# Value products in one piece behind an up group, both value copies ahead of the gelu

## The reference

```
h = layernorm(x) * (1 + ca) + sa
q = h @ w_dq.T @ w_uq.T;  k, v = split(h @ w_dkv.T @ w_ukv.T)      # 16 heads of 16
p = softmax(q @ k.T / 4 + causal mask)
x = x + ga * (p @ v) @ w_out.T
h = layernorm(x) * (1 + cb) + sb
expert 0: gelu(h @ W0a.T + b0a) @ W0b.T + b0b;  expert 1: relu(h @ W1a.T + b1a) @ W1b.T + b1b
x = x + gb * (the output of the expert with the larger gate score, token by token)
```

## Time and profile before

| | |
|---|---|
| three runs | 595.57, 596.92, 600.63 us; median 596.92 |
| profiled execution | 593.84 us, span of the trace 592.1 us |
| TensorE | 515.4 us busy (87%), 4912 matmuls |
| VectorE | 480.8 us (81%), 949 instructions |
| ScalarE | 366.5 us (62%), 521 |
| GpSimd | 311.9 us (53%), 300 |
| granted TensorE clock, mean | 0.951 |

### The profile page before, as it was taken

One profiled execution on the slowest core, in us unless ns is written; L12 is line 12 of the kernel. 1 busy time (PEld: TensorE's weight loads), 2 busy tenths in 40 slices (PEclk: granted clock), 3 DMA queues, 4 the chain that ended last, 5 costly groups with the idle time before them and its releaser, 6 DMA issues.

```text
span 592.1 us, 14257 instructions
## 1 busy us (share of the span) xinstructions
PE 515.4 (87%) x4912; PEld 446.2 (75%) x4912; DVE 480.8 (81%) x949; ACT 366.5 (62%) x521; POOL 311.9 (53%) x300
## 2 busy tenths in 40 slices
PE   4534685989999999999999999999999999999974
PEld 4424463788888988888888888788988898888874
DVE  3538163779999899989898989999899999887573
ACT  1524464858585866667676858585766667676320
POOL 6235232455656665755646565656665665552441
PEclk9856598899999999999999999999999999999998
DMA  8835453262707080716244351708080615210100
GB/s 246 206 46 76 50 74 75 52 95 37 128 18 145 2 161 3 121 42 90 71 68 93 50 111 31 130 7 154 0 152 13 108 39 91 55 39 2 37 19 18
DMA packets 43802, 43.74 MB, mean 74 GB/s; under 512 B 5344, under 2 KB 40800, under 8 KB 43760
## 3 DMA queue, kind: packets, MB, share of 16 engines
q1 hardware_dynamic: 43760, 43.19, 39.1%
HBM read 13.39 MB, written 4.23 MB: 30 GB/s over the span
## 4 chain that ended last, share of the span: by engine, by line
PE 49%; DVE 19%; DMA 10%; issue 9%; SPq 5%; POOL 3%; ACT 3%; DVEq 0%; POOLq 0%; ACTq 0%
DMA qs<-parts_q 8%; PE ps_s L382 6%; DVE mx L933 6%; PE ps_t L401 5%; PE ps_o L419 3%; PE ps_a L333 3%; PE ps_t L405 3%; SPq L282 3%; PE ps_a L334 3%; PE ps_a L335 3%; PE ps_c L333 3%; PE ps_c L335 2%; PE ps_c L334 2%; PE ps_o L333 2%; POOL xs L1186 2%
## 5 line engine op out<-in xcount | busy, mean ns | idle before, releaser
L794 ACT ACTIVATE score_rows<-ps_s 128x1024 f32<-128x1024 f32 x96 | 98.8, 1030 | 79.3 <-PE ps_s L382 66.2
L1246 POOL TENSOR_SCALAR_AFFINE_SELECT score_rows<-score_rows 128x512 f32<-128x512 f32 (+1 forms) x96 | 80.0, 834 | 110.4 <-ACT score_rows L794 109.8
L933 DVE TENSOR_REDUCE mx<-score_rows 128x4 f32<-128x1024 f32 (+1 forms) x96 | 114.6, 1210 | 5.7 <-POOL score_rows L1246 5.5
L806 ACT ACTIVATE p<-ps_t 128x1024 f32<-128x1024 f32 x96 | 98.5, 1026 | 17.9 <-PE ps_t L405 17.3
L382 PE MATMUL ps_s<-ks,qs 96*128 96x256 bf16 (+1 forms) x512 | 63.3, 260 | 33.2 <-DMA qs<-parts_q 29.7
L382 PEld LDWEIGHTS ps_s<-ks,qs 96*128 96x128 bf16 x512 | 37.0, 103 | 47.9 <-DMA qs<-parts_q 23.2
L1186 POOL TENSOR_TENSOR xs<-z,xs 128x512 f32<-128x512 f32 (+1 forms) x16 | 34.9, 2182 | 68.7 <-DVE z L1022 68.7
L401 PE MATMUL ps_t<-qs,ks 99*128 99x256 bf16 (+1 forms) x512 | 61.1, 254 | 11.0 <-DMA qs<-mx_rows 10.3
L401 PEld LDWEIGHTS ps_t<-qs,ks 99*128 99x128 bf16 x512 | 38.8, 101 | 17.5 <-DMA qs<-mx_rows 6.3
L405 PE MATMUL ps_t<-past_b,ident_b 128*128 128x256 bf16 (+1 forms) x192 | 46.0, 322 | 0.0
L1234 POOL TENSOR_TENSOR hid_lo<-hid,hid_hi 128x512 fp32r<-128x512 f32 x32 | 42.8, 1350 | 4.8 <-DVE hid_hi L1092 4.8
(11 more groups left out here) (166 smaller groups left out, 1631.4 us busy)
## 6 DMA issues: line engine op xcount, KB each, us to landing
qs<-parts_q SPq DMA_DIRECT2D x96, 128.0 KB, 4.0
ks<-parts_k SPq DMA_DIRECT2D x96, 128.0 KB, 4.7
xs<-x SPq DMA_DIRECT2D x16, 256.0 KB, 4.1
gates<-gates_scratch SPq DMA_DIRECT2D x16, 256.0 KB, 4.5
out<-xs SPq DMA_DIRECT2D x16, 256.0 KB, 2.9
p<-wmod SPq DMA_DIRECT2D x1, 1024.0 KB, 6.7
p<-waT SPq DMA_DIRECT2D x1, 1024.0 KB, 9.1
p<-wmod SPq DMA_DIRECT2D x1, 512.0 KB, 5.9
```

Of the source, the lines that this page charges most:

```text
L794: act.activation(score_rows[c % 2][:], ps_s[:], ACT.Copy).then_inc(scores_out, 1)
L806: act.activation((p0, p1)[tile][:, h0:h0 + n, :], ps_t[:].rearrange("p (h s) -> p h s", h=n), ACT.Exp, scale=SCALE).then_inc(exp_done, 1)
L933: dve.tensor_reduce(dst, score_rows[c % 2][:].rearrange("p (h k) -> p h k", h=n), AX_X, ALU.max).then_inc(max_done, 1)
L1246: pool.affine_select(out=diag, in_=diag, compare_op=ALU.is_ge, fill=NEG, base=0, pattern=[[0, n], [-1, P]], channel_multiplier=1).then_inc ...
```

## The change

- `values` becomes one stage of all 16 heads. It waits for v and for all six chunks of exponentials, and writes group g to columns g * 256 to g * 256 + 255 of the two banks of `ps_t`, instead of `ps_o`. `pv_done` counts 2 for a batch (after groups 1 and 3), before 4.
- On TensorE it stands behind `up(at(3), 0)`. Before, groups 0 and 1 stood on both sides of `s_chunk` 5 ahead of `expand_k`, and groups 2 and 3 behind up 0. `st_chunk` 0 of the next batch now also waits for both value copies (`o_ready`).
- On ScalarE `k_first` comes ahead of the copies, and both `values_copy` follow at the end of the step, so that the second one is ahead of the next step's `gelu` 0, which it followed before.
- The lists of users of `ps_o` are shortened, and its memset at the start goes away.

```diff
                 if c == 0:
                     pe.wait_ge(maxrows_in, 16 * (b.n + 1))
+                    wait(pe, o_ready, 2 * b.n)
...
-            def values(b, g, *users):
+            def values(b):
...
-                if g == 0:
-                    pe.wait_ge(v_ready, b.n + 1)
-                pe.wait_ge(exp_done, CH * b.n + ST_OF_GROUP[g])
-                bank_left(users)
-                for n in range(4):
-                    h = 4 * g + n
-                    dst = BANK["PVa"][32 * n:32 * n + HD + 1, (g % 2) * S:(g % 2 + 1) * S]
-                    pe.matmul(dst, v[b.parity][:, 0, h, :], p0[:, h, :], start=True, stop=False)
-                    mm = pe.matmul(dst[:, P:S], v[b.parity][:, 1, h, :], p1[:, h, :], start=False, stop=True)
-                mm.then_inc(pv_done, 1)
+                pe.wait_ge(v_ready, b.n + 1)
+                pe.wait_ge(exp_done, CH * (b.n + 1))
+                for g in range(4):
+                    for n in range(4):
+                        h = 4 * g + n
+                        dst = ps_t[32 * n:32 * n + HD + 1, g * S:(g + 1) * S]
+                        pe.matmul(dst, v[b.parity][:, 0, h, :], p0[:, h, :], start=True, stop=False)
+                        mm = pe.matmul(dst[:, P:S], v[b.parity][:, 1, h, :], p1[:, h, :], start=False, stop=True)
+                    if g % 2 == 1:
+                        mm.then_inc(pv_done, 1)
...
                 st_chunk(at(2), 5)
-                values(at(2), 0, ("DN0", at(4)), ("UP3", at(4)), ("V", at(1)))
                 s_chunk(at(1), 5)
-                values(at(2), 1)
                 expand_k(at(0), ("CKV", at(0)))
                 up(at(3), 0, ("Q", at(0)), ("T2", at(3)))
-                values(at(2), 2, ("PVa", at(2)))
-                values(at(2), 3)
+                values(at(2))
                 up(at(3), 1, ("DN1", at(4)), ("T1", at(0)))
...
             def step(at):
                 gelu(at(4), 0)
-                values_copy(at(3), 1)
                 maxima_rows(at(2))
...
                 scores_copy(at(1), 5)
+                k_first(at(0))
                 values_copy(at(2), 0)
-                k_first(at(0))
+                values_copy(at(2), 1)
                 rest_of_weights(at(0))
...
-            dve.memset(ps_o[:], 0.0).then_inc(blank, 1)
```

More of the change, by code:

```diff
@@ L210, in block_kernel @@
         BANK = dict(T1=ps_a, Q=ps_c, CKV=ps_b, K=ps_b, V=ps_o, MT=ps_c, OT0=ps_o, OT1=ps_b, AT=ps_b, OP=ps_c, T2=ps_c,
-                    GT=ps_a, GX=ps_b, UP0=ps_c, UP1=ps_a, UP2=ps_c, UP3=ps_o, DN0=ps_o, DN1=ps_a, PVa=ps_o, PVb=ps_o)
+                    GT=ps_a, GX=ps_b, UP0=ps_c, UP1=ps_a, UP2=ps_c, UP3=ps_o, DN0=ps_o, DN1=ps_a)
         LAGS = 4
@@ L340, in _ @@
                 "K": ((k1_ready, 1, 1), (kr_ready, 1, 1)), "V": ((v_ready, 1, 1),), "MT": ((mt_ready, 1, 1),),
-                "PVa": ((o_ready, 2, 1),), "PVb": ((o_ready, 2, 2),), "OT0": ((attn_ready, 2, 1),), "OT1": ((attn_ready, 2, 2),),
+                "OT0": ((attn_ready, 2, 1),), "OT1": ((attn_ready, 2, 2),),
                 "AT": ((a_hi_ready, 1, 1), (a_lo_ready, 1, 1)), "OP": ((gated_ready, 1, 1),), "T2": ((g32_ready, 1, 1),),
@@ L603, in _ @@
             pe.wait_ge(consts_ready, 6)
-            pe.wait_ge(blank, 4)
+            pe.wait_ge(blank, 3)
             pe.wait_ge(z1_ready, 1)
@@ L618, in step @@
                 turn_maxima(at(2), ("UP0", at(4)), ("Q", at(1)))
-                turn_values(at(3), 0, ("PVb", at(3)))
+                turn_values(at(3), 0, ("DN0", at(5)), ("UP3", at(5)), ("V", at(2)), ("OT0", at(4)))
                 turn_values(at(3), 1, ("K", at(1)), ("CKV", at(1)), ("GX", at(5)))
                 up(at(4), 2, ("MT", at(2)), ("UP0", at(4)))
-                expand_v(at(1), ("OT0", at(3)), ("PVb", at(3)), ("PVa", at(3)), ("DN0", at(5)), ("UP3", at(5)), ("V", at(2)))
+                expand_v(at(1), ("OT0", at(3)), ("DN0", at(5)), ("UP3", at(5)), ("V", at(2)))
                 gate(at(4), ("UP1", at(4)))
@@ L625, in step @@
                 st_chunk(at(2), 0)
-                up(at(4), 3, ("V", at(1)), ("OT0", at(3)), ("PVb", at(3)), ("PVa", at(3)), ("DN0", at(5)))
+                up(at(4), 3, ("V", at(1)), ("OT0", at(3)), ("DN0", at(5)))
                 project_out(at(3), ("UP2", at(4)), ("MT", at(2)))
@@ L685, in values_copy @@
                     return
-                act.wait_ge(pv_done, 4 * b.n + 2 * half + 2)
+                act.wait_ge(pv_done, 2 * b.n + half + 1)
                 wait(act, ot_done, 2 * b.n)
-                act.activation(oT[:, 2 * half:2 * half + 2, :], BANK["PVa"][:].rearrange("p (g s) -> p g s", g=2), ACT.Copy).then_inc(o_ready, 1)
+                act.activation(oT[:, 2 * half:2 * half + 2, :], ps_t[:, half * 512:(half + 1) * 512].rearrange("p (g s) -> p g s", g=2), ACT.Copy).then_inc(o_ready, 1)
             def second_expert(b, t):
@@ L763, in v_copy @@
                 act.wait_ge(v_done, b.n + 1)
-                wait(act, pv_done, 4 * (b.n - 1))
+                wait(act, pv_done, 2 * (b.n - 1))
                 act.activation(v[b.parity][:, :, :, 0:HD], BANK["V"][:].rearrange("p (t h e) -> p t h e", t=TT, h=NH), ACT.Copy).then_inc(v_ready, 1)
@@ L799, in exponentials @@
                 act.wait_ge(st_done, CH * b.n + c + 1)
-                wait(act, pv_done, 4 * (b.n - 1) + (2, 1, 2, 4, 3, 4)[c])
+                wait(act, pv_done, 2 * (b.n - 1) + (1, 1, 1, 2, 2, 2)[c])
                 if b.first and c == 0:
```

## The result

The changed kernel takes 622.2 us (median of 4 runs, 616.9 to 623.71) against 596.9: 1.040 times the kernel before, 95% interval 1.032 to 1.048, slower. The forecast was 612.9 and slower, with a range of 602 to 622: the direction is as forecast, and the time lies at the upper end of the range, 0.2 us beyond it. The profiled execution took 616.9 us, span 615.1, against 593.84: +23.1 us. The ten periods from the fourth start of mx_rows on are 33.58 us each on average, 31.87 before: +1.71 us.

The account below looks back on a forecast made before the run. VectorE's and TensorE's balanced loops were taken to bound the kernel, VectorE's stall deciding: 11.0 + 4.7 + 0.8 less 0.5 = +16.0 us, giving 609.8 profiled and 612.9 on the 596.92 median, range 602 to 622.

Parts of the forecast that it names:

- Two closed loops near each other: VectorE's round and TensorE's loop through mx_rows, SyncE's queue and s_chunk 0 are closed and balanced to some tenths.
- Part 1: Values in one piece behind up 0: up 0 starts at 304.43, up 1 0.47 us later, products end at 308.77.
- Part 2: Both value copies ahead of gelu 0: hidden_high(0) comes 7.46 us after q_rest instead of 6.08, so VectorE idles 1.38 us.
- rival D: A pause at ScalarE's table load: 1.28 us, 15 times, 19 us more, 632 us; chance 0.03.
- mx_rows is behind gelu 0 in the queue and starts 0.1 us before gelu's end: On ScalarE, mx_rows starts at about 311.55 instead of 310.51, moving s_chunk 0 by the same 1.04 us.
- The two loops are thus lengthened by 1.04 and 1.38 us; the longer decides: TensorE's loop grows 1.04 us, VectorE's 1.38; they are not added, and the longer sets the period.
- The five boundaries with a stall of 0.94 us: At five boundaries VectorE already waited 0.42 us for the last scores, so its stall is 7.46 - 6.52 = 0.94 us.
- 13 boundaries less 0.5: 8 x 1.38 = 11.0 and 5 x 0.94 = 4.7 us, less 0.5 for short VectorE waits on TensorE that go.
- 0.8 was taken: The last two boundaries with gelu, where VectorE was already waiting: 2 x 0.4 = 0.8 us.
- A (VectorE takes the stall back): No measurable change (597): a late VectorE misses holds by GpSimd and regains its stall within its round; chance 0.11.
- B (faster): About 591: entries saved, s_chunk 5 some 0.8 us earlier, no second wait on a copy; chance 0.05.
- C (more holds): About 624: the stall plus one more 0.9 us GpSimd hold of VectorE's casts in 13 periods, 12 us; chance 0.09.

Follow-up runs that it names:

- second copy back: The changed kernel with the second value copy put back behind gelu 0: 605.7 us, 1.014 times the kernel before.
- gelu 0 first: The changed kernel with gelu 0 ahead of both value copies, products still in one piece: 600.4 us, 1.008 times the kernel before.
- maxima in another bank: The changed kernel with the transposed maxima in ps_t instead of ps_c, ScalarE's order unchanged: 612.0 us, 1.026 times the kernel before.
- order alone: The kernel before with only ScalarE's order changed (copy of k, both value copies, then gelu 0): 612.3 us, 1.027.
- table ahead, tile last: The changed kernel with a two-column gelu loading the table ahead of both value copies, its result tile allocated last: 601.3 us, 1.008.
- s_chunk 5 ahead alone: The kernel before with only s_chunk 5 moved ahead of values 0: 596.9 us, 1.004.

## Why the prediction was right, and what it missed

- **Two closed loops near each other: right.** The loss came as waits, and the period grew by the delay of one chain, the one through mx_rows.
- **Part 1: right.** Up 0 starts 0.15 us behind q_rest (0.12 forecast), values another 1.60 us later (1.51), and four groups take 351.20 - 348.45 = 2.75 us (2.77). The idle time ahead of expand_k is 0.65 to 0.98 us in ten of its 13 cases (0.6 forecast).
- **Part 2: right.** 7.44 us from q_rest to hidden_high(0), 7.46 forecast; a stall of 1.36, 1.38 forecast. The load lies 0.02 us behind the copy and nothing drains. By rival D, or by the drain that the Trainium skill ("ScalarE: Activation LUTs", What ACT_TABLE_LOAD costs) counts with each switch, the stall would be above 2.6 us; the trace says no. The 1283 ns that the section gives for the load itself agree with the 1.28 us of each load here.
- **"mx_rows is behind gelu 0 in the queue and starts 0.1 us before gelu's end, ... +1.04 us": this failed.** It took only ScalarE's queue for the reason. The transpose that feeds mx_rows writes `ps_c`, in which up 0's result waits for gelu 0; `turn_maxima`'s first user is `("UP0", at(4))`, in the printed list. So gelu 0 ends, then come a hand-over of 0.1 us, 0.39 us until the transpose has passed on, and mx_rows: +1.70 instead of +1.04. With another bank mx_rows starts 0.1 us before gelu 0's end, as forecast.
- **"The two loops are thus lengthened by 1.04 and 1.38 us; the longer decides": the wrong loop was taken to decide.** The growth of the period was forecast as VectorE's stall. Cut at three points, the ten periods say otherwise (mean us; the first three columns add up to the period):

| kernel | q_rest's end to mx_rows | mx_rows to s_chunk 0 | s_chunk 0 to q_rest's end | period | q_rest's end to hidden_high(0) |
|---|---|---|---|---|---|
| before | 6.18 | 8.87 | 16.82 | 31.87 | 6.14 |
| the change | 7.89 | 8.87 | 16.83 | 33.58 | 7.47 |
| second copy back | 6.59 | 8.88 | 16.96 | 32.42 | 6.17 |
| gelu 0 first | 6.50 | 8.87 | 16.82 | 32.19 | 6.05 |
| maxima in another bank | 7.29 | 8.90 | 16.86 | 33.05 | 7.47 |
| order alone | 7.38 | 8.96 | 16.85 | 33.19 | 6.96 |
| table ahead, tile last | 6.53 | 8.87 | 16.88 | 32.28 | 6.09 |

- In every one of these kernels most of the growth lies in the first column, the way to mx_rows; the other two columns move by 0.14 us at most. VectorE's delay, the last column, is another number: the period grew by 0.3 to 0.6 us in three kernels where VectorE was not late by more than 0.03, and with the other bank it grew by less (1.19) than VectorE was late (1.33). So VectorE had some slack, which the prediction denied. That the forecast 612.9 is near the 612.0 of that kernel is luck in part: its 1.21 us a period were meant as VectorE's stall, which measures 1.33, and what lengthened the period was mx_rows with 1.11, for which 1.04 had been worked out and set aside. No kernel has the stall without a late mx_rows, so what the stall would cost alone stays open.
- **The five boundaries with a stall of 0.94 us: misread.** One was read, and the others were taken to be like it because the load stands directly behind the copy of k there too. The 0.42 us wait for the last scores is in that one alone. The first of the five has a longer wait and yet only 4.91 us from q_rest to hidden_high(0), and the other three have none. At the one just before 464 us it is 437.78 - 431.71 = 6.07 us in the kernel before, as at the other boundaries:

```profile
431.02 0.69 DVE L984 TENSOR_TENSOR rest_q<-ps_c,parts_q 128x512 f32<-128x512 f32 x1
...
437.78 0.41 DVE L1092 CAST hid_hi<-hid 128x512 fp32r<-128x512 f32 x1
```

- After the change the 13 waits are 2.77 us for the first and between 1.26 and 1.49 for the other twelve.
- **The 9.3 us between 612.9 and 622.2.** In the profiled executions it is 616.9 against 609.8. Up to the 15th mx_rows (501.16 before, 521.58 now) 20.4 us were lost where 13 boundaries less 0.5 made 15.2; behind it 2.6 where 0.8 was taken. The other 2.2 us are the step to the median, 5.3 us here and 3.1 in the runs before. By the periods, the bank's 0.53 us is worth 6.9 us of this in 13 periods.
- **Rivals.** A (VectorE takes the stall back): no. The cast of the maxima is indeed shorter, 303 ns on average against 889, but the two instructions ahead of it are longer, and the four instructions of the split take 35.4 us in all against 35.9: the hold has only moved, and it lies before the stall. B (faster): s_chunk 5 ahead alone gives nothing. C (more holds): not seen either, VectorE's busy time is 478.3 against 480.8 us; that the time came out near its 624 has another cause.

## What to carry to other kernels

Before a step is moved behind another on an in-order engine, follow its result to every reader and also to everyone who waits for its buffer: here the second list led to the loop that sets the period, and it could be read in the code. When two loops are close to each other, cut the period at points of both and see in which part it grows; a long wait on an engine does not by itself say that the period has grown by it. Here a table load was free where the engine waited anyway and cost about its full length, 1.30 us a period, where it stood between a late input and a waited-for output; either keep the function that needs it ahead of late copies, or load the table in an idle time by a tiny call. When a small edit adds a tile, allocate it last, or its experiment measures the shifted tiles too.

## What the runs showed of the hardware that was not expected

In the kernel before, an unused tile of 8 bytes among the constants, which moves all tiles behind it by 32 bytes a partition, made the DMAs land later: the k stack from 4.7 to 5.4 us (128 KB), the gates from 4.5 to 5.8, the DMA engines' share for the same 43.19 MB from 39.1 to 44.4% of the span, and the kernel slowed by 3.4%. The x tile is allocated first and did not move, yet its loads went from 4.1 to 5.4 us and the stores from it from 2.9 to 4.7. All of them pass through one queue, so a landing time does not tell which transfers are slow by themselves. Counted from the list of tiles, the stacks lie at a multiple of 64 bytes before (115712) and not after it (115744). That the multiple of 64 is what counts was not tried with other shifts; moving the gate tiles and the small ones behind them by 32 bytes, from 224480 to 224512, changed nothing that could be measured (gates 4.4 us).
